# Attention with a mixture of experts on one core: adding the causal mask of one-head pieces on VectorE, inside the row maximum

## What is computed

```python
S = einsum('hid,hjd->hij', K, Q) * SCALE        # rows by K, columns by Q
delta = idx[:, None] - idx[None, :]
decay = where(delta < 0, 0.0, -delta)
S = where(delta < 0, -inf, S) + decay
C = softmax(S, axis=-1)
attn = einsum('hij,hjd->hid', C, V)
```

## The kernel before

| tile | pieces (index) | heads in one | width of one head |
|---|---|---|---|
| 0 | 1 (0) | 4 | 128 |
| 1 | 2 (1, 2) | 2 | 256 |
| 2 | 4 (3 to 6) | 1 | 384 |
| 3 | 4 (7 to 10) | 1 | 512 |
| 4 | 4 (11 to 14) without diagonal, 1 (15) | 1, 4 | 512, 128 |
| 5 | 4 (16 to 19) without diagonal, 2 (20, 21) | 1, 2 | 512, 256 |
| 6 | 4 (22 to 25) without diagonal, 4 (26 to 29) | 1, 1 | 512, 384 |
| 7 | 4 (30 to 33) without diagonal, 4 (34 to 37) | 1, 1 | 512, 512 |

## Time and profile before

### The profile page before, as it was taken

How to read it: one execution, slowest core, us unless ns; L and a number is a source line. 1 busy time by engine, 2 the same in 40 slices (tenths; PEclk the granted TensorE clock), 3 DMA queues, 4 the chain that set the end, 5 groups by cost and what they waited for, 6 DMA issues and landing times.

```text
span 801.9 us, 16763 instructions
## 1 busy us (share of the span) xinstructions
PE 748.2 (93%) x5578; PEld 448.8 (56%) x5579; DVE 534.3 (67%) x1084; ACT 520.7 (65%) x1044; POOL 298.5 (37%) x342
## 2 busy tenths in 40 slices
PE   4999998999999999999999999999989999999894
PEld 2555553444544544554544544544438899999673
DVE  2456878788777777787787787787404544444287
ACT  3775556576666676676676676676786566666354
POOL 1342232252242553454343453434134457444300
PEclk9999999999999999999999999999999999999988
DMA  8789935254465575476475566495555755555496
GB/s 229 216 205 267 250 127 127 34 107 97 98 120 110 112 140 122 100 145 126 91 146 123 94 144 131 97 219 96 121 93 168 195 179 166 159 168 164 139 298 240
DMA packets 87302, 119.54 MB, mean 149 GB/s; under 512 B 16207, under 2 KB 60751, under 8 KB 87167
## 3 DMA queue, kind: packets, MB, share of 16 engines
q1 hardware_dynamic: 76686, 94.54, 51.0%
q0 software_dynamic: 10544, 24.07, 11.1%
HBM read 72.65 MB, written 45.55 MB: 147 GB/s over the span
## 4 chain that ended last, share of the span: by engine, by line
PE 69%; DVE 9%; DMA 8%; issue 7%; ACT 3%; POOL 2%; SPq 1%; ACTq 0%; POOLq 0%; DVEq 0%
PE ps L1394 16%; PE ps L1331 14%; PE ps L1380 13%; PE ps L1474 7%; PE ps L1496 7%; DVE mxa L981 6%; DMA arena<-y_dram 3%; PE ps L1383 3%; PE ps L1334 3%; DMA aug<-q_parts 2%; PE ps L1292 2%; PE ps L1457 2%; DMA q_parts<-arena 2%; POOL arena L646 2%; ACT arena L872 1%
## 5 line engine op out<-in xcount | busy, mean ns | idle before, releaser
L981 DVE TENSOR_REDUCE mxa<-ps 128x1 f32<-128x512 f32 (+3 forms) x608 | 363.0, 657 | 93.6 <-PE ps L1334 62.5
L872 ACT ACTIVATE arena<-ps 128x512 f32<-128x512 f32 x576 | 311.9, 604 | 148.8 <-PE ps L1383 128.6
L1331 PE MATMUL ps<-aug 105*128 105x512 bf16 (+3 forms) x768 | 228.8, 327 | 13.3 <-DVE mxa L981 9.2
L1380 PE MATMUL ps<-aug 108*128 108x512 bf16 (+3 forms) x768 | 216.2, 327 | 2.0 <-ACT arena L872 0.8
L1394 PE MATMUL ps<-arena,v_q 128*32 128x512 f32 (+3 forms) x1536 | 140.4, 491 | 3.7 <-ACT arena L872 3.7
L1331 PEld LDWEIGHTS ps<-aug 105*128 105x128 bf16 x768 | 74.8, 98 | 82.6 <-DVE mxa L981 34.2
L1380 PEld LDWEIGHTS ps<-aug 108*128 108x128 bf16 x768 | 66.1, 98 | 83.4 <-issue 32.5
L1383 PE MATMUL ps<-maskT_sb,idb 128*128 128x128 bf16 x512 | 112.4, 220 | 0.0
L1334 PE MATMUL ps<-mask_sb,idb 128*128 128x128 bf16 x512 | 98.6, 219 | 0.0
L778 POOL DMA_INDIRECT y_dram<-arena,y_row_of x71 | 68.6, 966 | 74.3 <-DVE arena L1231 72.8
L754 POOL DMA_INDIRECT xs_dram<-arena,slot x64 | 62.0, 969 | 76.8 <-ACT arena L872 38.1
(11 more groups left out here) (132 smaller groups left out, 715.9 us busy)
## 6 DMA issues: line engine op xcount, KB each, us to landing
aug<-k_parts SPq DMA_DIRECT2D x96, 128.0 KB
aug<-q_parts SPq DMA_DIRECT2D x96, 128.0 KB
arena<-xs_dram SPq DMA_DIRECT2D x71, 128.0 KB, 2.1
arena<-y_dram SPq DMA_DIRECT2D x16, 512.0 KB, 4.9
k_parts<-arena SPq DMA_DIRECT2D x16, 384.0 KB, 4.3
q_parts<-arena SPq DMA_DIRECT2D x16, 384.0 KB, 3.4
arena<-in_x SPq DMA_DIRECT2D x8, 512.0 KB, 5.9
xn_dram<-arena SPq DMA_DIRECT2D x8, 512.0 KB, 7.5
```

What stands on the lines that cost most here:

```text
L872: nc.scalar.activation(probs[SLOT[k, u]][:, half], score_bank(q, i), ACT.Exp).then_inc(exp_done, 1)
L981: nc.vector.tensor_reduce(mxa[:, h:h + heads, col_], src, AX.X, ALU.max).then_inc(piece_used, 1)
L1331: ins = nc.tensor.matmul(out_, k_aug[n][0:SCORE_ROWS, h0 + h, ib * P:(ib + 1) * P], q_aug[n][0:SCORE_ROWS, h0 + h, lo:lo + width], start=T ...
L1380: ins = nc.tensor.matmul(out_, q_aug[n][0:ALL_ROWS, h, jb * P:(jb + 1) * P], k_aug[n][0:ALL_ROWS, h, i0:i0 + hi - lo], start=True, stop=lo ...
```

## The change

Pieces of one head that hold the diagonal (tiles 2, 3, 6 and 7: 16 of the 38 pieces) get no mask matmul. VectorE adds a mask as wide as the piece (zeros, then the 128 mask columns) in the operation that takes the maximum, and writes the sum back into the bank. For tiles 6 and 7 that operation starts from the maximum of the first part, read from `mxa`, so the two parts needn't be merged; `split_maxima` merges only tiles 4 and 5. Zeros and mask lie side by side in a buffer `blank`, so one view serves all widths. VectorE waits for the constants before the pieces beside the projections, and for the zeros.

```diff
+def masked_by_vector(piece):
+
+    ib, lo, h, heads, width = PIECES[piece]
+    return heads == 1 and lo + width == P * (ib + 1)
+
+
+MERGED = len({ib for piece, (ib, lo, *_) in enumerate(PIECES) if 0 < lo and not masked_by_vector(piece)})
...
-        zeros = sb("zeros", [P, D])
+        blank = sb("blank", [P, D + P // 2])
+        zeros = blank[:, 0:D]
+        wide_mask = blank[:, :].bitcast(bf16)
+        mask_sb = wide_mask[:, 2 * D:2 * D + P]
...
-                nc.vector.tensor_reduce(mxa[:, h:h + heads, col_], src, AX.X, ALU.max).then_inc(piece_used, 1)
+                if masked_by_vector(piece):
+                    row = banks[:, 0:width]
+                    begin = NEG
+                    if lo > 0:
+                        dve.wait_ge(piece_used, s - HQ + PIECE_BANKS + 1)
+                        begin = mxa[:, h, TB // 2 + ib:TB // 2 + ib + 1]
+                    nc.vector.tensor_tensor_reduce(
+                        out=row, in0=row, in1=wide_mask[:, 2 * D + P - width:2 * D + P], scale=1.0, scalar=begin,
+                        op0=ALU.add, op1=ALU.max, accum_out=mxa[:, h, ib:ib + 1]).then_inc(piece_used, 1)
+                else:
+                    nc.vector.tensor_reduce(mxa[:, h:h + heads, col_], src, AX.X, ALU.max).then_inc(piece_used, 1)
...
-                nc.vector.tensor_tensor(mxa[:, :, TB // 2:TB], mxa[:, :, TB // 2:TB], mxa[:, :, TB:],
-                                        ALU.max).then_inc(m_step, 1)
+                split, merged = slice(TB // 2, TB // 2 + MERGED), slice(TB, TB + MERGED)
+                nc.vector.tensor_tensor(mxa[:, :, split], mxa[:, :, split], mxa[:, :, merged], ALU.max).then_inc(m_step, 1)
...
             ahead_of_windows = iter(list(enumerate(stream(0))))
+            dve.wait_ge(zeros_set, 1)
+            dve.wait_ge(consts_in, 16 * NCONST)
...
-                    diagonal = lo + width == P * (ib + 1)
+                    diagonal = lo + width == P * (ib + 1) and not masked_by_vector(piece)
```

More of the change, by code:

```diff
@@ L232, in attention_moe_kernel @@
         idb = sb("idb", [P, P], bf16)
-        mask_sb = sb("mask_sb", [P, P], bf16)
         maskT_sb = sb("maskT_sb", [P, P], bf16)
@@ L409, in many_zeros @@
         def many_zeros(n):
-            return bass.AP(zeros[:, :].tensor, zeros[:, :].offset,
-                           [list(zeros[:, :].ap[0]), [0, n], [1, D]])
+            return bass.AP(zeros.tensor, zeros.offset, [list(zeros.ap[0]), [0, n], [1, D]])
         best, first, second, gap, gexp, where, norm, low = col
@@ L433, in _ @@
                      "wv": (wvg_sb[:, :, 0:D], weights(wvT)), "gate": (wvg_sb[:, :, D:D + E], weights(gate)),
-                     "idb": (idb[:, :], ident_b), "mask": (mask_sb[:, :], mask_neg),
+                     "idb": (idb[:, :], ident_b), "mask": (mask_sb, mask_neg),
                      "maskT": (maskT_sb[:, :], mask_negT), "before": (before_sb[:, :], before),
@@ L636, in _ @@
             pool.sem_inc(split_done, 8)
-            nc.gpsimd.memset(zeros[:, :], 0.0).then_inc(zeros_set, 1)
+            nc.gpsimd.memset(zeros, 0.0).then_inc(zeros_set, 1)
             for n in range(AUG):
@@ L723, in clear_pads @@
                     nc.gpsimd.indirect_dma_start(
-                        out=xs_dram, in_=zeros[:, :], in_offset=None,
+                        out=xs_dram, in_=zeros, in_offset=None,
                         out_offset=bass.IndirectOffsetOnAxis(ap=pad_slot[:, e:e + 1], axis=0)).then_inc(xs_zero, 16)
@@ L1052, in _ @@
                     chunk(b, c, (B - b) * CHUNKS - c - 1, next_items(CHUNKS * (b - PLAIN) + c))
-            dve.wait_ge(consts_in, 16 * NCONST)
             step = [0]
@@ L1333, in send_piece @@
                     if diagonal:
-                        ins = nc.tensor.matmul(out_[:, width - P:], idb[:, :], mask_sb[:, :], start=False, stop=True)
+                        ins = nc.tensor.matmul(out_[:, width - P:], idb[:, :], mask_sb, start=False, stop=True)
                 ins.then_inc(piece_done, 1)
```

## The result

The changed kernel takes 817.69 us (median of 4 runs, 810.36 to 823.83), the kernel before beside it 803.87; the ratio is 1.0128 [1.0078, 1.0177]. It is slower, as forecast, and 813.0 was 4.7 us short of the median of four and 2.0 short of that of three. The profiled execution took 815.0 us (span 813.2), against 803.67 before: 11.3 us more, and these are split up here.

A forecast was written before the change was run, and what follows sets the result against it. VectorE's reductions through three banks, not TensorE at 93%, were taken to bound the windows. Stretches add 11.4 us, three windows with transfers take off 1.7: +9.7 on 803.67 gives 813.4, stated as 813.0 by the median; range 800 to 830.

The forecast's parts named there:

- The bound: TensorE is busy 93%, but in the windows VectorE, through three banks, decides; 15.0 us is the most to gain.
- stretches 1 and 2: Steps between batches of value products, pieces 4 to 12 and 26 to 34; forecast +0.21 and +0.32 us.
- The recursion: TensorE may write piece n when VectorE has reduced piece n-3; starts and bank releases give each stretch's end.
- Stretch 3: Pieces 35 to 37, the split of the maxima, pieces 0 to 3 of the next group; forecast +0.26 us.
- term A: Price per changed VectorE reduction of delivering the maximum as a second result: 0.07 us taken, ends 0 and 0.155.
- term b: Price of the running maximum from a pointer, in tiles 6 and 7: 0.06 us per reduction, low end 0.
- rival (d): Total time within the noise, with term A of 0.01 to 0.02 us; chance 4%.
- (e): The forecast itself, 813.0 us, with term A from 0.05 to 0.11 us; chance 64%.
- Rival (c): VectorE's read and write in one bank take turns: 0.4 to 0.53 us more per piece, some 870 us; chance 3%.
- Three windows with a late transfer: TensorE waits about a microsecond at piece 0 for q parts, so stretches 2 and 3 cost nothing there: -1.7 us.
- The clock: The clock granted in the windows should stay at 1.00.
- The projections: 24 changed pieces go beside TensorE work: 0 taken, between -1.4 and +2.2 us.

The follow-up runs named there:

- the cheap form: The changed kernel without the pointer and, in the windows, with VectorE's sum written to SBUF instead of the bank; 846.41 us, ratio 0.9982 to the kernel before.

## Why the prediction was right, and where only its total was

**The bound, right.** TensorE's 93% was no measure of what its products are worth: 256 of them out, 15.0 us by count, are worth 3.7 us in the windows with VectorE's new work in place, and 7.8 with none. VectorE in the stretches, through the three banks, is what sets the end. The sign rests on that, and on the price of VectorE's operation: with the cheap form stretches 1 and 2 are shorter than before.

**The recursion, right.** With the measured 0.515 and 0.65 for the distances and 0.85 from start to free bank (0.65 to the read, 0.14, 0.06), stretch 1 comes to 0.65 + 3 x 0.515 + 2 x 0.65 + 0.85 + 0.31 = 4.66, measured 4.63. For the cheap form it gave 4.39 and 4.22, measured 4.38 and 4.23. Stretch 3 follows it less well, because it hasn't the casts' meeting with GpSimd in it: 5.34 was given, and 5.35 or 5.42 came.

**The term A (second result), mis-sized.** 0.07 was taken; its parts are 0.01 for the addition with its read and 0.04 for the write into PSUM that I had put at 0, so 0.05 in distance, and the read's 0.14 that delays a bank. The price of a short instruction behind another wasn't the right row: the read runs beside the next main one. **The term b (pointer)** is right by itself (0.67 against 0.61), but it was added to A, and in fact it hides the 0.04: 0.67 and 0.54 instead of 0.73 and 0.60. Per stretch: +0.10, +0.07 and +0.16 where +0.21, +0.32 and +0.26 stood. 11.4 us was forecast for the steady part and 4.7 came; in the forecast's own formula, -1.6 + 186A, that is an A of 0.034, between rival (d) and the lower end of (e): none of the cases to which I gave a chance. Rival (c), read and write in one bank taking turns, had the right place for a cost, at a tenth of its size (0.04 instead of 0.4 to 0.53).

**Three windows with a late transfer, wrong in sign.** I took 1.7 off, because a wait for q parts would cover the loss. In windows 2 and 4 it does. But in sum these waits grew, from 3.7 to 9.6 us on TensorE's products, and one drew a half-clock spell of 3.4 us after it: some 5.5 us, in windows 3, 10 and 12.

**The clock, wrong.** I expected 1.00 in the windows. The steady ones have it (window 331 us: 1.00), but window 3 has 0.72 (241 to 247 us), and the mean over runs falls by 0.0041 with the change.

**The projections, small.** The part ahead of the windows is 1.6 us shorter; 0 was taken, and the low end was -1.4.

So the steady part came out at less than half, and 5.5 in the windows and 2.3 behind them, neither foreseen, made the total nearly right. That is luck: the range held because of ends that were put there for other reasons. What was sound is the mechanism and its sign; in the forecast for what to look for, "waits of the weights for VectorE grow by over 15" came (26.6), "distances 0.73 and 0.60" did not.

**Open.** Why transfers for q parts are late, in window 3 with the change and elsewhere by other amounts from chip to chip and run to run; what ScalarE and VectorE wait for on the slowest chip; why the output takes the 2.3 us behind the windows; and why the kernel with masks on both engines loses so much less in time than in its undisturbed stretches.

## What to carry to other kernels

Work moved off an engine with a 90% share is worth what its stretches show, not what the count says: write out, per stretch and through the number of buffers, who ends last, and do it with the distances of starts. If VectorE must add and reduce in one operation, let it write the sum to SBUF and not back into PSUM, and do without a pointer; merge the columns later in one small instruction. And when TensorE gets less to do, look at its granted clock and at the waits for transfers over a dozen runs before a gain of half a per cent is believed.

## What the runs showed of the hardware

- A VectorE operation that also delivers an accumulator has a read of 0.14 us (0.08 when its main result goes to SBUF) that starts with the next main instruction; with the addition it costs 0.01 us of distance (0.61 against 0.598). The Trainium skill's 60 ns of fixed overhead on SBUF ("Perfetto Trace Analysis", section "Optimizing Scalar/DVE Operations"), by which the prediction priced an alternative, isn't what the read adds; the measurement decides.
- The same operation writing 512 values to PSUM instead of SBUF stands 0.04 us further from the next (0.65 against 0.61); a first value from a pointer costs 0.06, and not both (0.67).
- A VectorE cast of 128x32 takes 0.40 instead of 0.18 us when it starts 0.54 us after an indirect transfer's start on GpSimd; those that start between 0.52 and 0.75 all end 0.93 or 0.94 after it.
- After a wait of 2.39 us TensorE was at the lower clock level 1.4 us later; after one of 2.57 us in the same profile the clock stayed at 1.00. With 16 of 32 masks per group out of TensorE the mean clock of the span fell by 0.0041 (0.0018); with 16 products of zeros a window it was 0.0020 (0.0020) above before's.
- The same kernel takes 803.9 to 849.3 us from chip to chip (medians). On the fastest and the slowest, the two with a profile of it as it stands, the undisturbed stretches are equal (4.53, 4.40, 5.41). What the slowest has more is waits of ScalarE and VectorE (25.0 and 17.9 us) for something that the profile can't name, waits of TensorE for nothing that it shows, and spells at half clock, not waits for q parts (2.8 against 3.1 us).
